# A two-layer decoder on one core: the first layer's front as one stream over four sequences, woven by a table with the rear of the group before

## The reference

```python
x = x + _L0_attn_ref(_layernorm(x, axis=-1), ...)            # stage A
x = x + _L0_xattn_ref(_layernorm(x, axis=-1), ctx_512, ctx_512, ...)   # stage B
x = x + _L0_ffn_ref(_layernorm(x, axis=-1), ...)             # stages C and D
...
# A: q = tanh(x @ W_charge.T + b_charge); shell = normalized x @ W_shell.T + b_shell
#    proj = shell @ omega.T + rff_bias; phi_s = [cos(proj), sin(proj)]
#    phi = (powers of q times phi_s) @ W_combine.T
#    logits = phi @ phi.T * T / temp, causal; out = softmax(logits) @ V @ W_out.T
# B: scores = (x @ Wq) . (ctx @ Wk), softmax over 361, times (ctx @ Wv)
# C: h = layernorm(x); 16-head causal attention of 16 channels a head; times wo
# D: h = layernorm(x); 8 experts, each token takes the best 2 (512 hidden, silu)
```

## Time and profile before

| | us |
|---|---|
| median of three runs | 1693.62 |
| lowest and highest | 1688.9, 1701.72 |
| the profiled execution | 1689.45 |
| its span, first to last instruction | 1687.8 |
| mean granted TensorE clock over the span | 0.857 of full |

### The profile page before, as it was taken

One profiled execution on the slowest core, in us unless ns is written; L12 is line 12 of the kernel. 1 busy time (PEld: TensorE's weight loads), 2 busy tenths in 40 slices (PEclk: granted clock), 3 DMA queues, 4 the chain that ended last, 5 costly groups with the idle time before them and its releaser, 6 DMA issues.

```text
span 1687.8 us, 24678 instructions
## 1 busy us (share of the span) xinstructions
PE 1285.4 (76%) x7936; PEld 890.2 (53%) x7936; DVE 998.3 (59%) x2156; ACT 522.3 (31%) x1279; POOL 415.1 (25%) x528
## 2 busy tenths in 40 slices
PE   2677868767877699981458977779787697986987
PEld 1554654644644366651237754467554475644755
DVE  4447557457455233325676765768656686677852
ACT  2214324324322222210125512346213363233620
POOL 1032143243253200006622111311212212032100
PEclk9778878878888799995679989779897799987988
DMA  9510010191014211101315310044100350104501
GB/s 376 217 28 1 19 28 13 34 408 49 25 46 198 59 47 44 44 29 45 117 39 98 86 40 12 10 101 111 40 12 2 86 122 21 32 11 88 114 5 46
DMA packets 69693, 122.37 MB, mean 73 GB/s; under 512 B 25404, under 2 KB 55100, under 8 KB 68032
## 3 DMA queue, kind: packets, MB, share of 16 engines
q1 hardware_dynamic: 63936, 110.04, 21.7%
q0 software_dynamic: 5632, 10.77, 2.3%
HBM read 67.69 MB, written 53.07 MB: 72 GB/s over the span
## 4 chain that ended last, share of the span: by engine, by line
PE 46%; issue 24%; DVE 12%; POOL 8%; DVEq 3%; ACT 3%; DMA 2%; POOLq 2%; SPq 0%; ACTq 0%
PE ps L1143 7%; PE ps L1390 5%; PE ps L1162 3%; PE ps L525 3%; PE ps L1316 3%; PE ps L1332 3%; PE ps L533 2%; POOL experts L1779 2%; PE ps L1302 2%; PE ps L1403 2%; PE ps L933 1%; PE ps L1041 1%; POOL headbd L681 1%; PE ps L504 1%; DVE probs L1999 1%
## 5 line engine op out<-in xcount | busy, mean ns | idle before, releaser
L1628 ACT ACTIVATE probs<-ps,small 100x361 f32<-100x361 f32 x256 | 141.3, 557 | 94.1 <-DVE small L2347 89.5
L2347 DVE TENSOR_REDUCE small<-ps 100x2 f32<-100x722 f32 x128 | 115.7, 906 | 36.2 <-PE ps L1302 36.2
L1143 PE MATMUL ps<-every,xT_t 128*128 x256 | 122.3, 601 | 0.4 <-issue 0.4
L1390 PE MATMUL ps<-hT,experts 128*128 128x400 f32 x288 | 117.1, 558 | 1.2 <-DVE small L730 1.2
L1316 PE MATMUL ps<-cst,probs 100*121 100x100 f32 x768 | 104.0, 271 | 8.1 <-DVE probsT L2355 7.7
L1316 PEld LDWEIGHTS ps<-cst,probs 100*121 100x121 f32 x768 | 94.8, 185 | 22.2 <-issue 13.7
L2355 DVE TENSOR_SCALAR probsT<-ps 121x600 f32<-121x600 f32 x128 | 99.2, 775 | 9.1 <-PE ps L1316 9.1
L1332 PE MATMUL ps<-probsT,values_ 121*32 121x100 f32 x1536 | 90.8, 253 | 0.9 <-DVE probsT L2355 0.9
L1302 PE MATMUL ps<-k_stack,q_stack 96*100 96x362 f32 x256 | 81.8, 400 | 6.3 <-ACT probs L1628 5.6
L473 POOL TENSOR_TENSOR small<-small,cst 100x2 f32<-100x2 f32 x56 | 11.1, 198 | 295.3 <-DVE small L453 295.2
L1390 PEld LDWEIGHTS ps<-hT,experts 128*128 128x128 f32 x288 | 59.6, 215 | 42.2 <-issue 14.1
(11 more groups left out here) (329 smaller groups left out, 2887.2 us busy)
## 6 DMA issues: line engine op xcount, KB each, us to landing
k_stack<-key_d SPq DMA_DIRECT2D x192, 90.5 KB, 3.1
tok_d<-wt SPq DMA_DIRECT2D x1, 14848.0 KB, 45.5
res_d<-wt SPq DMA_DIRECT2D x1, 14848.0 KB, 42.0
every<-e_d SPq DMA_DIRECT2D x8, 1536.0 KB, 11.6
ctxT<-ctxT_d SPq DMA_DIRECT2D x8, 726.0 KB, 4.3
key_d<-k_hi SPq DMA_DIRECT2D x32, 181.0 KB, 2.8
key_d<-k_lo SPq DMA_DIRECT2D x32, 181.0 KB, 3.4
gates<-gate_d SPq DMA_DIRECT2D x28, 200.0 KB, 4.4
```

Of the source, the lines that this page charges most:

```text
L1143: ins = e.matmul(ps[:, 2 * i + t % 2, :], xT_t[:, t % 2, c, :], every[:, bass.ds(base + (i * DC + c) * HID0, HID0)], start=(c == 0), stop= ...
L1390: ins = e.matmul(bank(2 * i + j % 2, n=NT), w[:, c, :], hT[:, c, :], start=(c == 0), stop=(c == DC - 1))
L1628: ins = e.activation(f_e[:, n % 2, i, 0:LC], bank(2 * (n % 2) + i, S, LC), ACT.Exp, bias=h_nm[:, n % 2, i:i + 1], accum_out=h_sum[:, b, h: ...
L2347: inc(e.tensor_reduce(h_nm[:, n % 2, 0:2], ps[0:S, 2 * (n % 2):2 * (n % 2) + 2, 0:LC], AX, ALU.max, negate=True), "F_nm")
```

## The change

Every function of the first layer that worked on a half gets a form for the whole group. `early(g)` is one stream with the same 18 steps, each over four sequences and all four banks 0 to 3. The signals of halves become signals of wholes (`wholes`); in the second layer, which still works in halves, the semaphores are the same with other bases. `behind` has 28 steps instead of 36: its steps outside `attend` are whole (4 before it, 5 behind it), the 19 of `attend` are the same. `woven(front, rear)` goes through a table: one front step, then one or two rear steps. The table puts one rear step behind each of the front steps 0 to 5, 10 and 16, and two behind each of the others. So `attend` starts behind front step 4 and ends behind step 14, where before it ran from round 3 to round 12. The first reciprocals of the attention (`recips_pool`) move into `attend` at n == 12. Front 0 is issued as `list(early(0))`, without a second stream. SyncE waits for the whole-group signals.

```diff
-ROUNDS, STEPS = 18, 19
+REAR_STEPS = (1, 1, 1, 1, 1, 1, 2, 2, 2, 2, 1, 2, 2, 2, 2, 2, 1, 2)
+STEPS = 19
...
-def woven(x0, x1, y):
-
-    for _ in range(ROUNDS):
-        for st in (x0, y, x1, y):
-            next(st)
+def woven(front, rear):
+
+    for steps in REAR_STEPS:
+        next(front)
+        for _ in range(steps):
+            next(rear)
...
+        def wholes(name, phase1, phase3="", sem_name=None):
+
+            sem = ctx.enter_context(nc.semaphore(sem_name or name))
+            for i, p in enumerate(phase1):
+                names[f"{p}_{name}"] = Signal(sem, len(phase1), i)
+            for i, p in enumerate(phase3):
+                names[f"{p}_{name}"] = Signal(sem, 2 * len(phase3), len(phase1) * NG + 2 * i, 2)
...
+        def norm4_dve(e, pre, g, src, xn_out):
+
+            stats, mv, _, r1, _, _ = for_y if pre in ("C_", "D_") else for_x
+            for b in range(NB):
+                e.bn_stats(stats[:, b, :], src[:, b, :])
+            e.drain()
+            for b in range(NB):
+                ins = e.bn_aggr(mv[:, b, :], stats[:, b, :])
+            inc(ins, pre + "mv")
+            e.drain()
+            yield
+            W(e, pre + "rstd", g)
+            for b in range(NB):
+                ins = e.tensor_scalar(xn_out[:, b, :], src[:, b, :], mv[:, b, 0:1], r1[:, b:b + 1],
+                                      ALU.subtract, ALU.mult)
+            return ins
+
+        def root4_pool(e, pre, g, eps2=None):
+
+            _, mv, var_e, r1, r2, t1 = for_y if pre in ("C_", "D_") else for_x
+            W(e, pre + "mv", g)
+            e.tensor_tensor(var_e, mv[:, :, 1], cs("eps", S)[:, 0:NB], ALU.add)
+            e.drain()
+            ins = e.tensor_tensor(r1, var_e, cs("mhalf", S)[:, 0:NB], ALU.pow)
...
+        def turn4_pe(e, pre, g, name, b0, src, ready, half=0):
+
+            W(e, ready, g, 1, half)
+            for c in range(DC):
+                for b in range(NB):
+                    ins = e.transpose(ps[:, b0 + c, b * S:(b + 1) * S], src[:, b, c * P:(c + 1) * P], identS)
+            inc(ins, pre + name)
...
+        def projT4_pe(e, w, src, b0, name):
+
+            for m in range(DC):
+                for c in range(DC):
+                    ins = e.matmul(bank(b0 + m, n=NT), w[:, c, m * P:(m + 1) * P], src[:, c, :],
+                                   start=(c == 0), stop=(c == DC - 1))
+            inc(ins, name)
+
+        def proj4_pe(e, w, srcT, b0, name):
+
+            for b in range(NB):
+                for c in range(DC):
+                    ins = e.matmul(ps[0:S, b0 + b // 2, b % 2 * D:(b % 2 + 1) * D], srcT[:, c, b * S:(b + 1) * S],
+                                   w[:, c, :], start=(c == 0), stop=(c == DC - 1))
+            inc(ins, name)
...
-                W(e, "A_ang", g, 1, h)
-                inc(e.activation(a_trig[:, t], a_ang[:, t], ACT.Sin), "A_trig")
+                W(e, "A_ang", g)
+                inc(e.activation(a_trig, a_ang, ACT.Sin), "A_trig")
...
+                    if n == 12:
+                        recips_pool(e, "C_", g, 0, 1)
...
+                W(e, "C_out", g)
+                W(e, "C_xb", g)
+                e.tensor_tensor(y[:], pair(6), y[:], ALU.add)
+                e.drain()
+                norm = norm4_dve(e, "D_", g, y, xd)
+                next(norm)
+                yield
+                if routed:
+                    e.wait_ge(r_sent.sem, g * (2 * NB * 16))
+                inc((yield from norm), "D_xn")
+                e.tensor_tensor(group, group, y[:], ALU.add)
+                e.drain()
+                yield
...
-            in_turn(early(0, 0), early(0, 1))
-            woven(early(1, 0), early(1, 1), behind(0, False))
+            list(early(0))
+            woven(early(1), behind(0, False))
             with e.Fori(1, NG - 1) as g:
-                woven(early(g + 1, 0), early(g + 1, 1), behind(g, True))
+                woven(early(g + 1), behind(g, True))
             list(behind(NG - 1, True))
```

More of the change, by code:

```diff
@@ L397, in decoder @@
             sem = ctx.enter_context(nc.semaphore(f"A_{n}_F_{f}"))
[L398 to L403, removed]
-        for n in ("nm", "e", "p", "pTp", "pT", "oTp", "oT"):
[L405 to L411, removed]
+            names["A_" + n] = Signal(sem, 1)
+            names["F_" + f] = Signal(sem, per, NG)
+        stage("A_", {"rn": 1, "lg": 1})
+        for n in ("nm", "e", "p", "pTp", "pT", "oTp", "oT"):
+            wholes(n, "AB", "", "AB" + n)
+        stage("B_", {"kqTp": 1, "kqT": 1, "qbkp": 1, "qbk": 1, "s": 1})
         for n, per in (("xq", 4), ("xqTp", 4), ("xqT", 4), ("pp", 3), ("p", 3), ("ytp", 1), ("ssr", 1),
@@ new lines, in part4, with turn4_act @@
+        def part4(b0):
+            return ps[:, b0:b0 + 2, 0:NT]
+        def turn4_pe(e, pre, g, name, b0, src, ready, half=0):
[4 more added lines that the diff above has]
+            inc(ins, pre + name)
+        def turn4_act(e, pre, g, pname, name, b0, dst, scale=None, bias=None):
+            W(e, pre + pname, g)
+            if scale:
+                for c in range(DC):
+                    ins = e.activation(dst[:, c, :], bank(b0 + c, n=NT), ACT.Identity, scale=col(scale, c),
+                                       bias=col(bias, c))
+            else:
+                ins = e.activation(dst, part4(b0), ACT.Copy)
+            inc(ins, pre + name)
@@ L463, in norm_pool @@
         def norm_pool(e, pre, g, h, eps2=None, fold=False):
+            o = own(h)
             yield
[L466 to L471, removed]
             W(e, pre + "mv", g, 1, h)
@@ L1957, in early @@
                 yield
                 yield
-                W(e, "A_out", g, 1, h)
-                W(e, "A_xb", g, 1, h)
-                add_out(x, p, h)
-                inc((yield from norm_dve(e, "B_", g, h, x, xnX)), "B_xn")
+                W(e, "A_out", g)
+                W(e, "A_xb", g)
+                e.tensor_tensor(x[:], pair(0), x[:], ALU.add)
+                e.drain()
+                inc((yield from norm4_dve(e, "B_", g, x, xnX)), "B_xn")
                 yield
                 yield
-                W(e, "B_qbkp", g, 1, h)
@@ L2037, in behind @@
-                for h in range(2):
-                    W(e, "C_vp", g, 1, h)
-                    inc(e.tensor_scalar(c_v[:, own(h), :], tokens(5 + 2 * h), 1.0, None, ALU.mult), "C_v")
-                    yield
+                list(norm)
+                e.drain()
+                for b in range(NB):
+                    ins = e.tensor_scalar(xn[:, b, :], y[:, b, :], r2Y[:, b:b + 1], None, ALU.mult)
+                inc(ins, "C_xn")
+                next(ways, None)
+                yield
+                W(e, "C_vp", g)
@@ L2050, in behind @@
-                norms = [norm_dve(e, "D_", g, h, y, xd) for h in range(2)]
-                for h in range(2):
-                    W(e, "C_out", g, 1, h)
-                    W(e, "C_xb", g, 1, h)
-                    add_out(y, 5 + 2 * h, h)
-                    next(norms[h])
-                    yield
-                for h in range(2):
-                    if h == 0 and routed:
-                        e.wait_ge(r_sent.sem, g * (2 * NB * 16))
-                    inc((yield from norms[h]), "D_xn")
-                    e.tensor_tensor(xall[:, bass.ds(g * NB + HB * h, HB), :], group[:, own(h), :], y[:, own(h), :],
-                                    ALU.add)
-                    e.drain()
-                    yield
@@ L2065, in behind @@
-                for h in range(2):
-                    scores_dve(e, "D_", g, h, g_s[:, own(h), :], 5 + 2 * h)
-                    yield
+                W(e, "C_out", g)
+                W(e, "C_xb", g)
+                e.tensor_tensor(y[:], pair(6), y[:], ALU.add)
+                e.drain()
+                norm = norm4_dve(e, "D_", g, y, xd)
+                next(norm)
+                yield
+                if routed:
+                    e.wait_ge(r_sent.sem, g * (2 * NB * 16))
+                inc((yield from norm), "D_xn")
```

465 lines of the change are left out of this document (218 added, 247 removed).

## The result

The changed kernel takes 1752.98 us (median of 4 runs, 1748.8 to 1756.9) where the kernel before takes 1691.69 in the same session: 1.0351 times as long [1.0299, 1.0403], 3.5% slower. By medians that is 61 us (the ratio is taken from all runs of the session, not from the two medians). The profiled executions, 1755.44 and 1689.45, lie 66 apart.

The account below looks back on a forecast made before the run. Bound: TensorE's work plus hops of short chains through other engines, partly covered by other queued work. Front 0 +20, three woven passes +12 and last rear +4 gave +36: 1725.5 us profiled, 1729 as median, range 1698 to 1760.

Parts of the forecast that it names:

- rival (3): Slower still by TensorE's clock: a pass +12, front 0 +32, last rear +5, median 1767; chance 0.15 together with (4).
- Front 0: First front alone, nothing covering it: one chain of 92.1 us against 71.2, rounded to +20, bounds +14 and +32.
- A woven pass: Front with rear woven in, three times: stretches sum to +2.6, plus 1.4 for the clock: +4 each, bounds -3 and +10.
- the five stretches: One pass cut at front steps 2, 8, 11, 14: gains 3.3 and 2.0, then losses 1.8, 1.5 and 4.6 us.
- the last stretch: From front step 14 to the pass's end: 29.7 us against 22.8 + 2.3 for moved work, a loss of 4.6.
- D's normalization behind the add: End of a pass: the table puts it behind the front's last add, exposing a row of 6.3 us formerly hidden.
- the second stretch: Front step 2 to step 8: 41.0 us against 43.0 before at equal work, a gain of 2.0.
- Idle ahead of step 11: TensorE's wait before front step 11's turns in a woven pass: 4 to 5 us, where two halves waited 2.7 and less.
- Last rear: Last rear alone: tail as one chain 20.9 us against 15.8, its head gaining 1: +4, bounds 0 and +6.
- (1): Faster, turn-taking was the price: idle TensorE halves, each pass gains 15.6, total 1671; decides from 8 a pass; chance 0.1.
- (2): Nothing measurable: the late table covers better, a pass gains 2 to 13 us, paying for the ends: 1694; chance 0.2.
- (4): The change doesn't weave: a wait for a whole-group load or signal holds the rear back; chance 0.15 together with rival (3).

Follow-up runs that it names:

- c1: The changed kernel with TensorE's waits filled by small fp32 products into unused PSUM, 97 more in a pass; 1721.76 us, 1.0156 of the kernel before.
- c3: t1 with TensorE's waits filled by small unused products at places chosen for its own waits; 1686.86 us, 0.9989 of the kernel before.
- c2: The kernel before with TensorE's waits filled by small unused products, also in the last rear; 1678.11 us, 0.9945 of the kernel before.
- t7: t1 with one table place changed: the rear's output projection behind front step 15 instead of 14; 1729.31 us, 1.0229 of the kernel before.
- t1: The changed kernel with an early table: pairs from round 4, projection behind step 14, D's normalization before the front's last add; 1710.15 us, 1.0106 of before.
- c4: c2 without the fillings in the last rear alone; 1674.97 us, 0.9895 of the kernel before.

## Why the prediction was right in direction and short in size

**What the number owes to the range.** Measured 1752.98 against a forecast of 1729. It lies inside 1698 to 1760, but above the forecast's own top of 1750: only the widening of the range for rival (3) takes it in. That is luck, and the sum was short. The own range was also added up from other bounds than the pass has in its paragraph: three times -3 and +10 are -9 and +30, where the sum has -2 and +18; with those the top would be 1762. And +2.6 a pass and "125.2 before clock effects against 123.8", which is +1.4, do not agree, as the corrections for moved work don't cancel.

**The bound, and the prices.** Idle TensorE behind short chains was the right reading, and the merged operations cost what the rule of 0.15 us fixed and 1.05 ns a column said: an add of 1024 columns takes 1.23 (priced 1.23), the reduction of 1444 takes 1.66 (1.67), a ScalarE copy of 800 takes 0.84 (0.85). Of table loads there are seven where there were 13, as predicted, four and three of them in the groups by line of ScalarE over the first layer:

```profile
L1491 ACT ACT_TABLE_LOAD x4 | 5.1, 1283 | 0.1
L1540 ACT ACT_TABLE_LOAD x3 | 3.8, 1283 | 0.1
```

**Front 0: +20 predicted, +25.1 measured.** The chain added up to 92.1, and "I round to +20, as some small operations still overlap" was a rounding the wrong way. TensorE's work was put at "47.9", and is 52.2: the clock went from 0.74 to 0.70. 92.1 + 4.3 is 96.4, and 96.3 were measured. So the chain's length was sound and the clock was left out of it, though some of the agreement is luck: VectorE was put at 26.6 us and is busy for 24.6, so other terms were as much too small. c1 and c3, filled in front of A's turns and in the steps behind, take 91.4 and 92.1.

**A woven pass: +4 predicted, +12.5 measured.** The signs of four of the five stretches were right. Predicted and measured lengths of the new stretches are 13.5 and 14.0, 41.0 and 43.1, 21.2 and 23.4, 19.8 and 21.6, 29.7 and 35.0. The sum, 125.2, was meant before clock effects, and against it 11.9 are missing in the second pass. The step that failed is the one that followed: "Most of them are at the full clock, while TensorE would now idle some 38 us a pass in fewer and longer waits; I add 1.4". The idle time was well foretold (39.1 in the second pass), its price was not: c1 shows 9.0 us a pass to be had by filling the waits, c2 4.1 before. The difference, 4.9, is the estimate of what the change costs through the clock, not 1.4. Rival (3) had the mechanism and the size of the pass (+12), but not all of the price through it.

The second mis-sized term is the last stretch, 35.0 us instead of 29.7. Step 15 to the output projection was put at 9.4 (its parts, 2.75, 3.5 and 3.7, add up to 9.95) and took 11.8 (364.54 to 376.30): the projection, priced 3.7, ran at the half rate (5.63) behind its own wait (2.04). The row behind the front's last products was put at 6.3 and took 8.6 (381.52 to 390.14), with turns and scores at or near the half rate. For D's normalization behind the add, "a loss of 4.6" in a row of 6.3 us, the runs show 2.9 to 8.1. The prediction had the place. What it did not see is that the projection is the cover of B's softmax, since it costed this stretch as a sum of parts and never asked what the projection had stood beside. Moving the projection alone costs 7.3 (t7).

**Steps at the table's start.** The gain of 2.0 in the second stretch came out as nothing to speak of: 43.1 measured, against the 43.0 of before at equal work. t1 pays 3.3 there for more of the rear and gets it back, so here the late start only shifted work to a place where it was dearer: 2.2 to 4.1 a pass.

**Idle ahead of step 11: 4 to 5 predicted, 6.04 measured.** The missing us is VectorE's normalization, 2.59 instead of 1.4, for a reason given in the last section.

**Last rear: +4 predicted (0 to +6), +6.4 measured,** just over the bound. The chain was right in kind: from the first turns to the last score copy it takes 22.4 us (588.27 to 610.69), where 20.9 was its sum and 15.8 the time before. The granted clock of that tail is 0.58, which the sum had no term for.

**Later work.** I let it cost the same. It is 3.3 us shorter here, 5.8 to 12.8 in the other kernels with a merged side (1133.5 in c3 to 1140.5 in c1, of before's 1146.3), but 0.2 and 1.0 in c2 and c4. Set beside each other instruction by instruction, the traces show where much of it lies: twice in the second layer VectorE takes up the first reduction of a self-attention. Before and changed, the first of the two:

```profile
1049.25 0.99 DVE L631 TENSOR_REDUCE small<-ps 100x8 f32<-100x800 f32 x1 [5.99 <-issue]
...
1114.84 0.99 DVE L695 TENSOR_REDUCE small<-ps 100x8 f32<-100x800 f32 x1 [3.27 <-PE ps L661]
```

Before, it begins 5.39 us behind the start of the first score product, and the profile shows nothing that it waits for; in the changed kernel 2.70 us behind, released by TensorE. c2 and c4 have the same 6.0 there with nothing shown; in all eleven kernels with a merged side it is 3.1 to 4.4, with TensorE as the releaser. What holds VectorE there in the kernels with the old front and rear stays open. The change doesn't touch that code, so this gain came by luck.

**The rivals.** (1), that the turn-taking was the price: t1's passes gain 1.7, far from the 8 from which it decides; false. (2): the late table doesn't cover better than I priced it; false. (3) comes nearest for the passes with its +12, but gives all of it to the clock, where the runs give about 5 to the clock and the rest to the order; front 0 stayed under its 32. (4): the streams weave. The sum, 25.1 + 37.6 + 6.4 less 3.3, is 65.8 against the +36 forecast.

## What to carry to other kernels

When one in-order stream is spread among another, list for each step that starts a chain over other engines what TensorE does until the chain returns, and keep the largest independent piece of work for the longest of them; one displaced projection cost 7 us of 122 here, and 2 where something behind it was late anyway. Merging halves into wholes saves a fixed part per instruction and takes away each half's cover: where another stream is woven in by a fitting table, that is about even (122.3 against 124.0), and where none is it costs a third of the stage (first front) or a twelfth (last rear). A sum of parts needs a clock term of its own wherever TensorE's idle time grows, and a kernel with filled waits measures it directly.

## What was not expected of the hardware

**Products that compute nothing make the kernel faster.** In the kernel before, 1689.80 to 1674.97 us in the same session, with a clock of 0.87 to 0.91 in the woven passes instead of 0.83 to 0.85; but in the last rear alone the same fillings cost 4.0 us, and taken out there (c4) they leave 75.3. A filling that outlasts its wait delays what stands behind it in TensorE's queue; that this is what happened there is argued and not shown.

**VectorE stands still beside GpSimd.** In the timeline of the changed kernel, all engines, around two normalizations:

```profile
260.60 1.38 DVE L478 TENSOR_SCALAR experts<-xin,small 100x256 f32<-100x256 f32 x4 [0.17 <-issue]
261.90 3.06 DVE L478 TENSOR_SCALAR y<-xall,small 100x256 f32 x4
...
262.13 2.03 POOL L1728 TENSOR_TENSOR x<-xin,rows 100x1024 f32<-100x1024 f32 x1 [0.43 <-DVE experts L478]
...
331.43 1.51 POOL L1755 TENSOR_TENSOR headbd<-kT,cst 128x800 f32<-128x800 f32 x1
331.48 2.59 DVE L478 TENSOR_SCALAR experts<-x,small 100x256 f32<-100x256 f32 x4
```

The same four operations take 1.38 us with no other work of GpSimd beside them (in front 0, at 24.57), 3.06 with GpSimd's bias add beside them and 2.59 with its product. Both times VectorE ends 0.8 and 1.1 us behind GpSimd (264.96 after 264.16; 334.07 after 332.94), about as long as its last three operations take (1.38 for four), as if it had stood still until then. The Trainium skill, "SBUF — State Buffer", section "Who interferes with whom", says that a VectorE instruction in a mode that uses both its ports shares a pair of them with GpSimd, and that the one which issues first holds the pair for its whole instruction while the other is blocked. The ends of the two lengthened rows agree. The first row shows that not every pair costs: GpSimd takes a power of four columns from 260.54 to 261.70 beside it, and it takes its 1.38 all the same. In halves, GpSimd's additions were about half as long (1.09 to 1.14 us of 512 columns, against 2.03 of 1024), and a half's normalization took 0.73 to 0.74. No kernel was run with these operations kept apart.
